# A transformer block of local attention and routed experts: values projected first, norm steps spread, loads and fetches moved

## What is computed

```python
q, k, v = [split_heads(x @ W + b) for W, b in ((Wq, bq), (Wk, bk), (Wv, bv))]
ctx = local_attention(q, k, v)                       # window of 256 keys
idx = concat([0], top_k(norm(q), 62), [1023])
ctx[idx] = softmax(q[idx] @ k.T / sqrt(32)) @ v
```

```python
probs = softmax(xt @ Wg); e = argmax(probs); pos = count of earlier tokens of expert e
out = gate * expert_e(xt) if pos < 256 else 0
expert(x) = (silu(x @ W1) * (x @ W3)) @ W2           # 512 -> 704 -> 512
return out + shared(xt)
```

## Time and profile before

| what | us |
|---|---|
| runs, median of 3 (lowest to highest) | 863.87 (862.54 to 869.77) |
| the profiled execution | 856.99 |
| its span, first to last instruction | 855.3 |
| PE busy | 788.5 (92%) |
| DVE busy | 564.9 (66%) |
| ACT busy | 420.9 (49%) |
| POOL busy | 144.8 (17%) |
| DMA rate over the span | 190 GB/s |

### The profile page before, as it was taken

How to read it: one execution, slowest core, us unless ns; L and a number is a source line. 1 busy time by engine, 2 the same in 40 slices (tenths; PEclk the granted TensorE clock), 3 DMA queues, 4 the chain that set the end, 5 groups by cost and what they waited for, 6 DMA issues and landing times.

```text
span 855.3 us, 13848 instructions
## 1 busy us (share of the span) xinstructions
PE 788.5 (92%) x5060; PEld 658.2 (77%) x5060; DVE 564.9 (66%) x1199; ACT 420.9 (49%) x833; POOL 144.8 (17%) x225
## 2 busy tenths in 40 slices
PE   2989999989999998998998899799999999999994
PEld 1868878777777776776887787799999999886883
DVE  6554698468887565775488545277766666758565
ACT  2544353445656564766544344366656666622120
POOL 4100010420111112230235532000000000013132
PEclk9999999999999998999999899899999999999998
DMA  6797554976776779661268722656877876545444
GB/s 210 216 307 242 176 173 164 283 199 175 188 209 153 195 200 248 194 193 31 75 205 298 249 91 63 184 165 206 246 229 215 252 222 216 154 155 184 148 136 147
DMA packets 117444, 162.39 MB, mean 190 GB/s; under 512 B 17316, under 2 KB 65188, under 8 KB 117376
## 3 DMA queue, kind: packets, MB, share of 16 engines
q1 hardware_dynamic: 113792, 153.54, 59.7%
q0 software_dynamic: 3584, 7.97, 3.2%
HBM read 107.24 MB, written 55.05 MB: 190 GB/s over the span
## 4 chain that ended last, share of the span: by engine, by line
PE 64%; DVE 18%; DMA 7%; ACT 5%; issue 4%; POOL 1%; SPq 1%; DVEq 0%; POOLq 0%; ACTq 0%
PE bank L163 41%; PE wide L163 17%; PE wide L167 3%; DVE MX L160 3%; PE bank L167 3%; DMA XX<-scr_xd 2%; DMA H2A<-scr_oe,FG 2%; DVE SG L160 1%; DVE STC L275 1%; DVE CX L1446 1%; DVE SIL L149 1%; DVE GC L153 1%; DMA scr_xd<-H2A,FSI 1%; DMA scr_xd<-H2B,FSI 1%; DVE CX L154 1%
## 5 line engine op out<-in xcount | busy, mean ns | idle before, releaser
L163 PE MATMUL wide<-W2H,HH 128*128 128x512 f32 x352 | 116.5, 397 | 3.6 <-DVE CX L1446 3.4
L160 DVE TENSOR_REDUCE MX<-wide 128x1 f32<-128x192 f32 (+1 forms) x128 | 77.6, 646 | 20.5 <-PE wide L163 17.8
L157 ACT ACTIVATE PT<-bank 128x512 f32<-128x512 f32 x128 | 73.5, 593 | 30.7 <-PE bank L163 28.6
L149 DVE TENSOR_TENSOR SIL<-bank,SIL 128x256 f32<-128x256 f32 (+1 forms) x72 | 36.9, 512 | 73.0 <-ACT SIL L157 72.3
L157 ACT ACTIVATE SIL<-bank 128x256 f32<-128x256 f32 (+1 forms) x72 | 32.6, 453 | 105.3 <-PE bank L163 99.7
L163 PEld LDWEIGHTS wide<-W2H,HH 128*128 128x128 f32 x352 | 66.8, 190 | 19.4 <-DVE CX L1446 5.1
L163 PE MATMUL bank<-XT,W13H 128*128 128x256 f32 (+1 forms) x336 | 76.6, 322 | 0.0
L163 PE MATMUL wide<-W2L,HH 128*128 128x512 f32 x192 | 75.5, 393 | 0.0
L149 DVE TENSOR_TENSOR HH<-SIL,HH 128x256 fp32r<-128x256 f32 (+1 forms) x72 | 37.0, 514 | 45.5 <-ACT HH L145 35.8
L145 ACT ACTIVATE HH<-SIL 128x256 fp32r<-128x256 f32 (+1 forms) x72 | 35.2, 489 | 63.4 <-DVE SIL L149 62.6
L163 PEld LDWEIGHTS bank<-XT,W13H 128*128 128x128 f32 x336 | 55.0, 188 | 4.7
(11 more groups left out here) (234 smaller groups left out, 2011.3 us busy)
## 6 DMA issues: line engine op xcount, KB each, us to landing
R<-in_L_ffn_W_dram SPq DMA_DIRECT2D x48, 512.0 KB, 5.2
scr_q<-hl SPq DMA_DIRECT2D x16, 512.0 KB, 4.1
scr_k<-hl SPq DMA_DIRECT2D x16, 512.0 KB, 3.9
R<-in_L_ffn_sw_dram SPq DMA_DIRECT2D x12, 512.0 KB, 5.8
QSe<-scr_q SPq DMA_DIRECT2D x36, 128.0 KB, 4.0
KSe<-scr_k SPq DMA_DIRECT2D x36, 128.0 KB
scr_v<-vt SPq DMA_DIRECT2D x16, 272.0 KB, 2.1
R<-_attn_hidden_states_dram SPq DMA_DIRECT2D x16, 256.0 KB, 3.4
```

What stands on the lines that cost most here:

```text
L149: return do(e, lambda g: g.tensor_tensor(dst, a, b, op), after)
L157: return do("act", lambda g: g.activation(dst, src, fn, **kw), after)
L160: return do("dve", lambda g: g.tensor_reduce(dst, src, AXX, op), after)
L163: return do("pe", lambda g: g.matmul(ps, a, b, start=start, stop=stop, skip_group_check=True), after, mark=mark)
```

## The change

**Start.** Wv is loaded first, in four row pieces, and split at once (ACT high; low on POOL and DVE in turn). Before `proj_group(0)`, `values_begin(j)` makes the eight products of a tile with Wv's high part, `values_end(j)` the four with its low part; group 0 then has Q and K alone. The norm of tiles 0 to 3 is scaled by ACT. POOL's constants come after tile 3, `twice` is written by ACT, Wk is loaded later.

```diff
+            def split_wv(k, e_lo):
+                a = copy("act", WHL[2][0][:, k, :], wv_raw[:, k, :], [m_wv[k]])
+                b = tt(WHL[2][1][:, k, :], wv_raw[:, k, :], f(WHL[2][0][:, k, :]), ALU.subtract, [a, m_wv[k]], e=e_lo)
...
+            split_wv(0, "pool")
+            ln_turn(0)
+            split_wv(1, "dve")
+            split_wv(2, "pool")
+            split_wv(3, "dve")
+            values_begin(0)
+            ln_turn(1)
+            ln_mean(2)
+            ln_norm(2)
+            ln_mean(3)
+            values_begin(1)
+            values_end(0)
+            load_w(1, wk)
...
-                for j in range(4):
+                for j in range(4 if g4 else 0):
```

```diff
+            LAST_STEPS = {116: ((h_mean, 4),), 120: ((h_x1, 4), (h_mean, 5)),
+                          124: ((h_mean2, 4), (h_x1, 5), (h_mean, 6))}
...
-                    elif 8 <= i < 11:
-                        load_2(0, i - 8)
+                    elif i in (8, 9, 11):
+                        load_2(0, (8, 9, 11).index(i))
...
-                if g == 76:
-                    load_tile(0)
-                    load_tile(1)
+                if g in (73, 79):
+                    load_tile(g // 79)
...
             scatter_rows(7)
+            load_tile(SEQ // P)
```

```diff
-                    if q < 2:
-                        work()
-                    if q == 1 and m == 0:
+                    if q == 1 or q == 0 and m < 5:
                         work()
...
+                    def take(t, busy, ps, m_p):
+                        k_(t, busy, ps, m_p)
+                        if q == 1 and t == 1:
+                            prepare(2, 0)
+                            prepare(2, 1)
+
+                    def between(t0, m):
+                        if q == 0 and (t0, m) in ((0, 2), (2, 0), (2, 4)):
                             work()
-                    down(4, hr, take)
-                    if q == 1:
-                        prepare(2, 2)
-                        prepare(2, 3)
+                        if q == 1 and (t0, m) == (2, 4):
+                            prepare(2, 2)
+                            prepare(2, 3)
+                    down(pairs, hr, take, between)
```

```diff
-                            fetch(4 * g + m - 4, False)
+                            fetch(4 * g + 2 * m - 8, False)
+                            fetch(4 * g + 2 * m - 7, False)
...
-                        if t % 2 == 1:
-                            conclude(4 * g + t - 1)
+                        if t == 1:
+                            conclude(4 * g)
+                        if t > 0:
                             conclude(4 * g + t)
-                        if t < 2:
-                            fetch(4 * g + t + 2, False)
-                    down(4, hr, take)
+                    down(pairs[0:1] + [((2,), UP), ((3,), UP)], hr, take)
```

More of the change, by code:

```diff
@@ L539, in ln_work, with values_out, values_begin, values_end @@
                         fn(n - back)
+            def values_out(g4, j, pi, pb, m_p):
+                vi, vb, vfree = vtr.take()
+                m_v = tt(vb[:, :, 1:2 * HD + 1], pb[:, :].rearrange("p (h d) -> p h d", d=2 * HD),
+                         bvb[:, :].rearrange("p (h d) -> p h d", d=2 * HD), ALU.add, [m_p, m_bias] + vfree)
+                pj.busy[pi].append(m_v)
+                r0 = g4 * 512 + j * P
+                m_s = dma("sp", vtr.slots[vi], lambda g: g.dma_start(
+                    vd[r0:r0 + P, :], vb[:, :, :].rearrange("p h d -> p (h d)")), [m_v, m_vone])
+                vtr.busy[vi].append(m_s)
+                vstore.append(m_s)
+                return m_v
+            vopen = {}
+            def values_begin(j):
+                pi, pb, pfree = pj.take()
+                _, HTb, ready, _ = ht[0]
+                tile = ready[2 * j:2 * j + 2]
+                for k in range(4):
+                    for l in range(2):
+                        mm(pb[:, :], HTb[:, l, k, j * P:(j + 1) * P], WHL[2][0][:, k, :], k + l == 0, False,
+                           pfree + tile + [m_w["v", k][0]])
+                vopen[j] = (pi, pb)
+            def values_end(j):
+                pi, pb = vopen[j]
+                HTb = ht[0][1]
+                for k in range(4):
+                    m_p = mm(pb[:, :], HTb[:, 0, k, j * P:(j + 1) * P], WHL[2][1][:, k, :], False, k == 3,
+                             [m_w["v", k][1]], mark=(k == 3))
+                values_out(0, j, pi, pb, m_p)
             def go_on():
@@ L747, in sandwich @@
             qt_b0, kv_b0, fence_ps = [], [], []
-            for n in range(6):
-                ln_work()
-                if n >= 2:
-                    split_w(0, n - 2)
+            ln_mean(0)
+            ln_mean(1)
+            ln_norm(0)
+            ln_norm(1)
+            split_wv(0, "pool")
[11 more added lines that the diff above has]
+            load_w(1, wk)
+            ln_turn(2)
+            ln_norm(3)
+            ln_mean(4)
+            values_begin(2)
+            values_end(1)
+            ln_turn(3)
+            split_w(0, 0)
+            constants()
+            k0 = zero_rows()
+            values_begin(3)
+            values_end(2)
+            split_w(0, 1)
+            ln_norm(4)
+            ln_mean(5)
+            values_end(3)
+            split_w(0, 2)
+            split_w(0, 3)
+            tick_a[0] = 6
             for g4 in range(4):
@@ L1129, in slot_of @@
                         load_keys(2 * i + 4 + k // 6)
+                    if g == 0:
+                        stack_q(0, ST_)
                     local_scores(g // 4, k % 4)
@@ L1179, in slot_of @@
                         H_AT[at](t)
+                for fn, t in LAST_STEPS.get(g, ()):
+                    fn(t)
                 if g in (117, 120, 122, 125):
@@ L1224, in sandwich @@
             XT.busy.append(list(begun))
-            h2free += [list(begun) for _ in range(3)]
+            h2free += [list(begun) for _ in range(3)] + [begun + sc[-2:]]
             for c in OWN:
@@ L1269, in up, with down @@
                 return m_p, ready
-            def down(tiles, hready, take):
-                for t0 in range(0, tiles, 2):
-                    got = [DN.take() for _ in range(2)]
+            def down(groups, hready, take, between=None):
+                for tiles, ring in groups:
+                    got = [ring.take() for _ in tiles]
                     for m in range(6):
-                        for q in range(2):
-                            t = t0 + q
-                            di, ps, fr = got[q]
+                        for t, (di, ps, fr) in zip(tiles, got):
                             s = slice(t * P, (t + 1) * P)
```

202 lines of the change are left out of this document (108 added, 94 removed).

## The result

| | before | after |
|---|---|---|
| median, us | 863.45 (862.54 to 869.77, 4 runs) | 838.04 (836.16 to 845.27, 4 runs) |
| profiled execution / span, us | 856.99 / 855.3 | 837.23 / 835.5 |
| TensorE's mean granted clock | 0.981 | 0.982 |

The ratio of the times is 0.9706, with a 95% interval of 0.9632 to 0.978: 25.4 us less by the medians, 19.8 less by the two profiled executions. Forecast were 839.0 in a range of 830 to 855, and "faster by over 1%" with 0.90. The time was met; whether its terms were met is another question, and the stages answer it.

What follows compares the result with a forecast made beforehand. TensorE was taken as the bound, busy 92% of the span, with gains only in its idle and low-clock time. Terms summing to 24.7 us gave 832.3 profiled; the 6.9 distance to the median made 839, range 830 to 855.

Steps and rivals of the forecast that it cites:

- the sum of 24.7: Whole kernel: gains of 4.5 start, 3 maxima, 6.5 shared passes, 4.6 first expert, 0.5 second bank, 5.6 end, in us.
- the distance of 6.9: Whole kernel: the old median lay 6.9 us above its profiled execution, and the new one was forecast to do the same.
- 4.5 after K: Start, first group: tile 7's low part would come 4.5 us after K ends, leaving PE a wait of that size.
- The first rival: Start: V's products stay at the low clock throughout, start term −4.5 us, time 848; chance 0.14.
- the 60.1: Start: the second group begins at 60.1 against 64.64, with 2.2 us included for the clock's fall.
- S: Start: the term for the whole new start, a gain of 4.5 us, bounds −4.5 and +8.
- stack_q ahead of the first scores: nothing, since a store ends that wait: Maxima: moving stack_q ahead of the first scores gains nothing, bounds 0 to 1 us.
- The term of 3: Maxima: moving W2 and tile loads removes most of the wait and low clock near 335; 3 us, bounds 0 and 4.9.
- the 8 of the prediction: Shared passes: gross gain of 8 us, 4.1 from waits and 5.0 from the clock, about 1 of it overlapping.
- no fall of the clock in the shared down parts: Shared passes: a sign that would show the prediction right; no size given.
- Rival (2): Shared passes: VectorE carries the first pass, 43 against PE's 37, and the clock falls twice; −3 us, time 848; chance 0.15.
- the tail is 3.9: End: one tile's VectorE work, its root and hand-overs take 3.9 us against the old tail's 6.1; gain 2.2.

Runs made afterwards that it cites:

- e5: The changed kernel once more with no edit; median 832.06 us, ratio to the old kernel 0.9703.
- e3: Changed kernel with head 1's row of maxima stored ahead of the loads for head 3 and a store of V; median 838.65 us, ratio 0.9731.
- e4: Changed kernel with the third piece of W2 back at step 80 and both tile loads back at step 76; 839.3 us, one execution.
- e7: Changed kernel with stack_q late, tiles turned one call earlier, and the routing count behind the turned tile's low part; median 832.38 us, ratio 0.9693.
- e8: Changed kernel with seven buffers for the normalised tiles in place of eight; 836.23 us, one execution.
- e9: Changed kernel with the second norm's steps in their old places, eight buffers kept; median 836.42 us, ratio 0.9755.
- e10: Changed kernel with the first expert's tiles loaded and turned where the old kernel did, second bank kept; median 833.56 us, ratio 0.9708.
- e1: Changed kernel with stack_q(0) back behind the first local scores; 830.78 us, one execution.
- e2: Changed kernel with the whole start of the old one (constants, loads, order of V); median 842.63 us, ratio 0.9752.
- e6: Changed kernel with stack_q(0) behind the first local scores, timed over several runs; median 833.17 us, ratio 0.9711.
- e11: Changed kernel with the last pass in two pairs on two banks again, eight fetch buffers kept; median 838.12 us, ratio 0.9765.
- e12: Changed kernel with four fetch buffers as before, single tiles at the end kept; median 833.42 us, ratio 0.9708.

## Why the prediction came out right

The time and the class were right, at the start, the maxima, the first expert and the end in the main for the reasons given, in the shared passes partly by terms that cancel, and the sum of 24.7 is near the 25.4 of the medians (26.5 in the set of e5). The profiled pair gave only 19.8, because the old kernel's profiled execution was a quick one (6.5 us under its median) and the changed kernel's had the slow landing of e5's comparison; the distance of 6.9 that I kept for the changed kernel was really 0.8. So 839 was reached in that pair by two errors of 5 and 6 us that cancel, which is luck.

**Start.** "First tile ready at 9.6" was 9.81, "Q starts at 28.7" 29.33, the second group 58.78 for 60.1 with a wait of 3.63 for "4.5 after K". The first rival, V cold throughout, is refuted by the row at 15.59: between waits of 1.57 us eight products took 2.07. The Trainium skill (TensorE: Matmul & The Clock Gate, "HAM oscillation — how this bites in real kernels") has bursts of about 2 us that start low each time, but behind waits of 3 to 5 us. The prediction left the length of the waits out and so stretched this to its own of 1.3; here bursts of 2 to 4 us parted by 1.57 did not start low. What failed most is the charge for the clock behind tile 7's wait: I put 2.2 into the 60.1, but the products run slow from 58.78 to 65, which costs 1.2 × 0.5 + 5 × 0.47 = 3.0. Counted as the 60.1 was, the group starts at 58.78 + 3.0 = 61.8; of the 1.7 between them 0.8 is this charge, 0.6 Q's later start, the rest the way from Q to the wait. S is 2.8 in this pair and 3.5 by the mean of eleven executions, for 4.5.

**"stack_q ahead of the first scores: nothing, since a store ends that wait."** The reason was right, the bound "0 to 1" was not. The store ends the wait, but I took its landing for a constant. From its issue to the products it was 3.18 us in the old profile (186.24 − 183.06), and 3.2 to 5.2 in the twelve executions of the new kernels that keep its place (all but e3); the clock may fall on top, and the stretch from a to c is 103.2 to 108.4 with stack_q ahead. In this pair that costs 4.1, on average 1.9, both against the one old profile.

**Maxima.** The rest of the wait, forecast at under 1.5, is 0 at that row. The term of 3 was 4.1 in this pair; e4 brings back 3.2 us of waits, in one execution. The reason given, the bytes moved away from this store, fits the wait near 335, but waits of this kind come up at other rows with the loads moved (e5, e7, e8).

**Shared passes.** 5.9 for 6.5. The mechanism holds (e9), with the weight on the spacing and little on the buffer (e8). The gross gain is larger than the 8 of the prediction, which had overlooked the fourth old wait (1.18 at 450.94: 5.2 us of waits, not 4.1), and so are the charges. The backlog of VectorE is there as forecast, a wait of 1.32 in the first pass, but with the low clock behind it (0.67 in the window at 430) it costs 3.0, not 1. In e5, the same program, a second such wait follows, and the clock falls behind that one:

```profile
439.26 1.24 PE L163 MATMUL wide<-wghl,XT 128*128 128x16 f32 x8 [1.29 <-DVE STC L935]
```

```profile
440.00:445.00 5.00, 5.00 (x19) 4.24 (x19) 4.13 (x10) 2.67 (x6) 3.07 (x4) 0.66 0.67 240
```

The step that I missed stands at the very start of the pass. The first call does the logits of three tiles in a row:

```profile
410.11 0.26 PE L163 MATMUL wide<-wghl,WQL 128*128 128x16 f32 x1
...
412.68 0.26 PE L163 MATMUL wide<-wghl,WKL 128*128 128x16 f32 x1
412.79 0.75 PE L163 MATMUL bank<-WQL,WQH 128*128 128x512 f32 x1
413.34 0.63 PE L163 MATMUL bank<-WKL,WQH 128*128 128x512 f32 x1
```

24 products of 16 columns, then 128x512 products 0.43 us apart for 3.5 us: the clock falls with PE busy all the time, 1.7 us. All twelve executions with these steps show it; e9 and the old kernel, which have no such row of 24, do not. That the narrow products are the cause is likely but no run changed them alone. The sign "no fall of the clock in the shared down parts" came for the first down only: in this pass the falls are in the up part now, but the window at 515 (0.66) lies in the second down. Rival (2), VectorE carrying the first pass, had VectorE's steps right (9.73, 8.52 and 7.31 us for 9.5, 8.8 and 7.1), but PE waited only once, so the rest of the backlog was covered.

**First expert.** 2.5 ahead of it and 2.5 behind, for 4.6 and 0.5: 5.0 for 5.1. The loads are issued at 526.77 and the first product starts 6.8 us later, where it was 9.9; no fall behind it. e10 brings 3.7 of it back in its trace, not in its median. Partly given back: behind the routing's two small waits (0.73 and 0.71, the same in both kernels) the window at 515 is now at 0.66, 1.7 us; the old kernel kept its clock there, as did e1, e2, e3, e6 and e9, whose g to h is 18.9 to 19.8 for 20.5.

**End.** 6.2 for 5.6; 5.5 by e11, 3.8 without its fall of the clock. The split was wrong: "the tail is 3.9". VectorE and PE in the changed kernel:

```profile
817.73 0.75 DVE L1536 SCALAR_TENSOR_TENSOR H2B<-H2B,GK,wide 128x512 f32<-128x512 f32 x1 [0.74 <-DMA H2B<-scr_oe,FG]
...
824.43 0.39 PE L163 MATMUL bank<-W2H,HH 128*128 128x512 f32 x1
...
827.43 0.74 DVE L1536 SCALAR_TENSOR_TENSOR GC<-GC,GK,bank 128x512 f32<-128x512 f32 x1
...
830.55 0.69 DVE L149 TENSOR_TENSOR XX<-XX,GC 128x512 f32<-128x512 f32 x1
```

The last tile's products end at 824.8, and its combine starts 2.6 later, since VectorE is still at the tiles before: from the last product's end to the last addition it is 6.4, and was 5.7 in the old kernel. The "4 us" of the prediction's signs did not come; PE is simply done earlier. The end is VectorE's, four tiles without a gap but two roots: 13.5 us from the first combine to the last addition, 15.6 before. That is 2.1, and the forecast had counted it twice, once as PE's waits for a bank (2.1) and once as a tail (2.2). The missing 4.1 came before, where I had counted 1.3: waits of 0.93, 0.82, 0.46 and 0.84 of the old kernel are gone, 3.1 in all, the first two in front of transposes, and a new one of 0.77 for a part of W2 has come. The second bank for turned tiles may be the cause of the first two; no run took it away alone. The other 1.8 us are in no wait of the timeline and stay open.

## What to carry to other kernels

Cut both traces at instructions that they share, and give each stage its own forecast: a total can be met by errors that cancel. Before a stage's loss or gain is explained, run the same program again; here one small store's landing and the clock behind it moved a stage by 5 us, and a single execution (e1) decided for a theory that its repeat (e6) did not bear out. An experiment that brings a wait back can bring a fall of the clock with it that the old kernel never had (e11): take the two apart. Where PE's waits and VectorE's tail meet at the end, count the chain of the engine that finishes last, once.

## What the runs showed of the hardware

A 4 KB store behind some 1 MB of loads and stores was waited for 3.18 us after its issue in one execution and 5.15 in another of the same program (e5, after). The clock fell behind single waits of 3.67, 2.71 and 2.37 us (after, e4, e12). Behind shorter ones it fell or not: 1.46 in e5 and 1.83 in e4 kept it, 1.93 in e9, 1.66 in e11 and 1.29 in e5 lost it, and in e5 a wait of 1.32 earlier in the same pass did not. It also fell behind 24 products of 16 columns without any wait.

The low parts of Wv on POOL and on VectorE overlap at 10 us:

```profile
9.98 1.42 POOL L149 TENSOR_TENSOR WVL<-R,WVH 128x512 fp32r<-128x512 f32 x1 [0.29 <-ACT WVH L145]
```

```profile
9.59 0.68 DVE L149 TENSOR_TENSOR WVL<-R,WVH 128x512 fp32r<-128x512 f32 x1
10.46 1.50 DVE L149 TENSOR_TENSOR WVL<-R,WVH 128x512 fp32r<-128x512 f32 x1 [0.19 <-ACT WVH L145]
```

VectorE's second one takes 1.50 in place of 0.68 and ends 0.56 after POOL's: it seems to stand still until POOL is through. The Trainium skill (SBUF — State Buffer, "SBUF: two separate sides") says that the later of two such instructions is blocked until the first is through, and here the trace agrees; VectorE's takes 1.49 or 1.50 in the executions of e1, e3, e4 and e5 too. The other way round it is less clear: POOL's, which began under VectorE's first, took 1.42, where POOL's earlier one took 1.27. The prediction's "up to 2.5 us from S" did not come: the first low product of V starts only at 17.50, and VectorE's next instruction waits for ACT.
